# Turning v on VectorE and splitting the head scaling between ScalarE and GpSimd in a fused attention and mixture-of-experts layer

## The reference

```
def attn(x, W_qkv, W_out, s):               # x is (4, 512, 256), after a layer norm
    q, k, v = split(x @ W_qkv)              # 32 q heads, 8 k and v heads of 64
    q, k = rope(q), rope(k)
    a = q @ k.T / 8                         # per head, 512 x 512
    a = where((q_pos >= k_pos) & (q_pos < k_pos + 64), -inf, a)
    w = softmax(concat([a, sink]))[..., :-1]
    return (w @ v) @ W_out

x = x + attn(layernorm(x))
x = x + moe(layernorm(x))                   # 8 experts, top 2 of them, capacity 640
```

## Time and profile before

| what | value |
|---|---|
| median of 3 runs | 1060.13 us |
| lowest, highest | 1054.63 us, 1065.57 us |
| profiled execution, device time | 1057.24 us |
| its span, first to last instruction | 1055.5 us |
| mean granted TensorE clock | 0.993 of full speed |
| busy share: PE, DVE, ACT, POOL | 97%, 88%, 62%, 63% |
| one period (from one group's heads to the next group's) | 23.5 to 24.9 us |

### The profile page before, as it was taken

How to read it: one execution, slowest core, us unless ns; L and a number is a source line. 1 busy time by engine, 2 the same in 40 slices (tenths; PEclk the granted TensorE clock), 3 DMA queues, 4 the chain that set the end, 5 groups by cost and what they waited for, 6 DMA issues and landing times.

```text
span 1055.5 us, 32277 instructions
## 1 busy us (share of the span) xinstructions
PE 1024.9 (97%) x12943; PEld 720.9 (68%) x12943; DVE 926.8 (88%) x1967; ACT 655.0 (62%) x1671; POOL 665.1 (63%) x607
## 2 busy tenths in 40 slices
PE   7899999999999999999999999999988999999996
PEld 4466666666666666666666666666656999999995
DVE  6999999999999999999999999999985787777773
ACT  4666667666667766667776666776663555445551
POOL 6667776777666888666787777777752333333332
PEclk9999999999999999999999999999989999999998
DMA  3534544544333334333334334333424555555521
GB/s 112 142 108 118 137 131 140 132 112 135 93 83 83 96 99 111 99 104 81 80 95 114 100 103 121 98 83 96 119 70 162 119 119 123 117 123 124 101 46 21
DMA packets 155893, 112.10 MB, mean 106 GB/s; under 512 B 76480, under 2 KB 145152, under 8 KB 155616
## 3 DMA queue, kind: packets, MB, share of 16 engines
q1 hardware_dynamic: 137680, 90.03, 33.0%
q0 software_dynamic: 7296, 8.55, 4.8%
q10 hardware_dynamic: 10768, 11.46, 3.6%
HBM read 74.84 MB, written 21.83 MB: 92 GB/s over the span
## 4 chain that ended last, share of the span: by engine, by line
PE 56%; DVE 37%; issue 3%; ACT 1%; POOL 1%; DMA 1%; SPq 0%; POOLq 0%; DVEq 0%; ACTq 0%
PE bank L1586 22%; DVE probs_ring L1162 16%; DVE probs_t L1171 14%; PE bank L1562 10%; PE bank L1739 9%; PE bank L1750 6%; DVE heads_sb L1191 4%; PE bank L1753 3%; PE bank L1618 1%; PE bank L1508 1%; PE bank L1526 1%; PE bank L1533 1%; DVE neg_max L1162 0%; ACT probs_ring L862 0%; PE bank L1491 0%
## 5 line engine op out<-in xcount | busy, mean ns | idle before, releaser
L862 ACT ACTIVATE probs_ring<-probs_ring,neg_max 128x512 f32<-128x512 f32 x512 | 365.8, 717 | 210.3 <-DVE neg_max L1162 209.6
L1162 DVE CUSTOM_DVE_ANT_0 probs_ring<-bank,mask,sink_neg 128x512 f32<-128x512 f32 x512 | 360.1, 737 | 26.6 <-PE bank L1562 25.5
L1171 DVE STREAM_TRANSPOSE probs_t<-probs_ring 128x1024 f32<-128x1024 f32 x256 | 317.5, 1240 | 0.2 <-ACT probs_ring L862 0.2
L1562 PE MATMUL bank<-qk_st 64*128 64x512 f32 x1024 | 281.1, 625 | 11.9 <-DVE neg_max L1162 7.4
L1586 PE MATMUL bank<-probs_t,v_quads 32*64 32x256 f32 x8192 | 247.6, 381 | 0.1
L1586 PEld LDWEIGHTS bank<-probs_t,v_quads 32*64 32x64 f32 x8192 | 179.1, 132 | 76.5 <-issue 48.8
L691 POOL TENSOR_TENSOR chunk_sb<-chunk_sb,rope_sb 128x512 f32<-128x512 f32 (+1 forms) x94 | 120.0, 1276 | 103.9 <-issue 82.7
L810 POOL DMA_INDIRECT out<-expert_sb,slots x40 | 78.8, 1969 | 143.1 <-DVE expert_sb L1428 134.5
L1562 PEld LDWEIGHTS bank<-qk_st 64*128 64x128 f32 x1024 | 85.3, 186 | 77.4 <-DVE neg_max L1162 41.8
L696 POOL TENSOR_TENSOR qk_st<-chunk_sb,swap_sb 128x512 f32<-128x512 f32 (+1 forms) x94 | 120.2, 1279 | 7.4
L1618 PEld LDWEIGHTS bank<-wo_sb,heads_sb 64*128 64x128 f32 x992 | 96.1, 187 | 37.4 <-issue 29.2
(11 more groups left out here) (191 smaller groups left out, 1342.7 us busy)
## 6 DMA issues: line engine op xcount, KB each, us to landing
v_quads<-v_rows SPq DMA_DIRECT2D x128, 128.0 KB
recip_wide<-recip_rows SPq DMA_DIRECT2D x64, 256.0 KB
w_raw<-in_L_ffn_w SPq DMA_DIRECT2D x14, 1024.0 KB, 7.6
swap_sb<-chunk_sb SPq DMA_DIRECT2D x314, 32.0 KB
w_raw<-in_L_attn_W_qkv SPq DMA_DIRECT2D x32, 256.0 KB, 2.9
slot_rows<-x2T ACTq DMA_DIRECT2D x8, 662.5 KB, 5.8
slots_cut<-slot_rows SPq DMA_DIRECT2D x56, 80.0 KB, 3.0
w_raw<-in_L_attn_W_qkv SPq DMA_DIRECT2D x64, 64.0 KB, 2.7
```

What stands on the lines that cost most here:

```text
L862: nc.scalar.activation(probs[(g * UNITS + n) % RING][:, :], probs[(g * UNITS + n) % RING][:, :], ACT.Exp, bias=neg_max[j][:, n:n + 1], sca ...
L1162: nc.vector.tensor_tensor_reduce(probs[(g * UNITS + n) % RING][:, :], SCORE[SCORE_OF[n // 2][n % 2]][:, :], mask[:, L - P - t * P:2 * L - ...
L1171: nc.vector.transpose(probs_t[j][:, :, (h // 2) * (2 * P):(h // 2 + 1) * (2 * P)] .rearrange("p b (h q) -> p h b q", h=2)[:, :, :, t * BLK ...
L1562: nc.tensor.matmul(SCORE[SCORE_OF[n // 2][hh]][:, :], qk_st[j][half, h // 2, t * P:(t + 1) * P], qk_st[j][half, PAIRS, :], start=True, sto ...
```

## The change

Five things change in each period.

1. v is no longer turned by four PE transposes and copied by ACT. DVE turns it with one block transpose (`turn_v`, step -7, i.e. 9 of the period before) from `chunk_sb` into the unused upper half of `swap_sb[KV]`. The trip through DRAM now writes 1024 pieces of 32 floats in two DMAs, where it wrote 128 rows of 256 floats in one, and reads back rows of 1024 floats.
2. The heads of all groups but the last leave PSUM by four ACT copies; POOL then multiplies them by the broadcast reciprocals, in two instructions of 128 x 512. Each of the two lets one half of the heads go.
3. The rotation of Q01 on POOL is cut in two: the products stay at step 5 and the sum goes to step 10, behind the scaling of the heads.
4. y0 on PE begins with the first half of the heads and waits for the second half in its middle. The residual sums on POOL move from step 38 (6 of the period) to steps 42 and 43 (10 and 11).
5. The scatters on POOL go three at a time at r = 99 and 115 (step 3 of a period, ahead of the rotation of k), and the last two at 127, for the third batch at 118.

```diff
-        TURN_V_AT, V_NEXT_AT = -8, -7
-        ROT_AT = {2: Q23, -12: KV, -11: Q01}
+        TURN_V_AT = -7
+        ROT_AT, Q01_TIMES_AT, Q01_SUM_AT = {2: Q23, -12: KV}, -11, -6
...
-        Y_FIRST_OUT_AT, Y_OUT_AT, RESIDUAL_AT = 30, 31, 38
-        ODD_ORDER = (1, 0)
+        Y_FIRST_OUT_AT, Y_OUT_AT = 30, 31
+        RESIDUAL_AT = {42: 1, 43: 0}
...
-        SCATTER_AT = {89: (0, 1), 99: (2,), 105: (3, 4), 115: (5,), 121: (6, 7)}
-        ROUTE_STEPS = 122
+        SCATTER_AT = {99: (0, 1, 2), 115: (3, 4, 5)}
+        LAST_SCATTERS, LAST_SCATTERS_AT = (6, 7), (127, 127, 118, 127)
+        ROUTE_STEPS = 128
...
-                sp.dma_start(v_rows, v_next[:, :, :].rearrange("p t d -> p (t d)")).then_inc(s_v_out, 16)
+                for q in range(HD // BLK):
+                    sp.dma_start(v_rows.rearrange("j (b d) -> j b d", d=HD)[:, :, q * BLK:(q + 1) * BLK],
+                                 v_turned[q * BLK:(q + 1) * BLK, :].rearrange("j (b i) -> j b i", i=BLK)
+                                 ).then_inc(s_v_out, 16)
...
+                if n == HEADS_AT and g < GROUPS - 1:
+                    pool.wait_ge(s_recip_in, g * 32 + 32)
+                    for half in range(2):
+                        part = slice(2 * half, 2 * half + 2)
+                        pool.wait_ge(s_heads_raw, 2 * g + half + 1)
+                        nc.gpsimd.tensor_tensor(heads_sb[:, part, :], heads_sb[:, part, :], recip_wide[:, part, :],
+                                                ALU.mult).then_inc(s_heads, 1)
...
+                if n == HEADS_AT and g < GROUPS - 1:
+                    act.wait_ge(s_pv, g + 1 + 1)
...
+                    for a in range(QUADS):
+                        ins = nc.scalar.activation(heads_sb[:, a, :], PV[a][:, 0:2 * P], ACT.Copy)
+                        if a % 2 == 1:
+                            ins.then_inc(s_heads_raw, 1)
...
+            def turn_v(g):
+                dve.wait_ge(s_chunk_out, g * CHUNKS + KV + 1)
+                if g > 0:
+                    dve.wait_ge(s_v_out, g * 32)
+                nc.vector.transpose(v_turned, chunk_sb[KV][HD:P, :]).then_inc(s_v_turned, 1)
...
-                if n == HEADS_AT:
+                if n == TURN_V_AT and g > 0:
+                    turn_v(g)
+                if n == HEADS_AT and g == GROUPS - 1:
...
-                    pe.wait_ge(s_heads, 2 * g + (half if g == GROUPS - 1 else 1) + 1 + 1)
+                    pe.wait_ge(s_heads, 2 * g + half + 1 + 1)
...
+                            if half == 0 and second == 1:
+                                pe.wait_ge(s_heads, 2 * g + 1 + 1 + 1)
```

More of the change, by code:

```diff
@@ L437, in chunk_bank @@
             return PV[3] if c == KV else PV[1] if c == Q23 and g == 0 else PROJ
-        def turned_v_bank(g):
-            return PV[0] if g == 0 else PROJ
         def turned_bank(half, last):
@@ L689, in rotate, with rotate_sum @@
                 straight, swapped = chunk_sb[c][rows, :], swap_sb[c][rows, :]
-                base = before_group + (q - Q23) * ROT_STEPS
                 nc.gpsimd.tensor_tensor(straight, straight, rope_sb[rows, 0, :], ALU.mult).then_inc(s_pool, 1)
                 nc.gpsimd.tensor_tensor(swapped, swapped, rope_sb[rows, 1, :], ALU.mult).then_inc(s_pool, 1)
-                pool.wait_ge(s_pool, base + 2)
+            def rotate_sum(g, j, c):
+                q = g * CHUNKS + c
+                rows = slice(0, HD) if c == KV else slice(0, P)
+                pool.wait_ge(s_pool, before_group + (q - Q23) * ROT_STEPS + 2)
                 if q == Q23:
                     pool.wait_ge(s_rot, Q23)
-                nc.gpsimd.tensor_tensor(qk_st[j][rows, PAIRS if c == KV else c - Q01, :], straight, swapped,
-                                        ALU.add).then_inc(s_rot, 1)
+                nc.gpsimd.tensor_tensor(qk_st[j][rows, PAIRS if c == KV else c - Q01, :], chunk_sb[c][rows, :],
+                                        swap_sb[c][rows, :], ALU.add).then_inc(s_rot, 1)
             pool.wait_ge(s_small_in, 16)
@@ L703, in pool_step @@
                     rotate(g, j, c)
+                if n == Q01_TIMES_AT and g > 0:
+                    rotate_times(g, Q01)
+                if n == Q01_SUM_AT and g > 0:
+                    rotate_sum(g, j, Q01)
                 if n == (SECOND_SPLIT_AT if g == 1 else SPLIT_AT) and 0 < g < GROUPS - 1:
@@ L763, in pool_route @@
                                    channel_multiplier=1).then_inc(s_ids, 1)
-                for c in SCATTER_AT.get(r, ()):
+                for c in LAST_SCATTERS if r == LAST_SCATTERS_AT[b] else SCATTER_AT.get(r, ()):
                     if not last:
@@ L841, in chunk_out @@
                     act.wait_ge(s_rot, q - CHUNKS + 1)
-                if c == Q23 and g > 0:
-                    act.wait_ge(s_v_turned, g + 1)
+                if c == KV and g > 0:
+                    act.wait_ge(s_v_turned, g)
                 nc.scalar.activation(chunk_sb[c][:, :].rearrange("p (c a i) -> p a c i", a=QUADS, i=BLK),
@@ L992, in act_ahead @@
                     act.wait_ge(s_late, 1 if i < TPB else 2)
[L993 to L994 removed]
+                    if i > 0:
+                        act.wait_ge(s_norm_turned, TPB + i)
+                    nc.scalar.activation(xn1[:, :], x_sb[:, TPB + i, :], ACT.Identity,
                                          bias=bias_late[:, i:i + 1], scale=rstd_late[:, i:i + 1]).then_inc(s_norm, 1)
@@ L1487, in project @@
                 else:
-                    pe.wait_ge(s_v_next, g + 1)
+                    pe.wait_ge(s_chunk_out, g * CHUNKS + Q01 + 1)
+                    if g % NKV == 3 and g > NKV:
+                        pe.wait_ge(s_x2T, 2 * (g // NKV))
+                    if g % NKV == 4 and g > NKV:
+                        pe.wait_ge(s_centred, g // NKV)
+                    if g % NKV == 5 and g > NKV:
+                        pe.wait_ge(s_place, g // NKV)
+                    if g - 1 in LATE_PERIODS:
+                        pe.wait_ge(s_xT_lo, TPB + LATE_PERIODS.index(g - 1) + 1)
                 for kc in range(KC):
@@ L1513, in project_pair @@
                                 ins.then_inc((s_proj_part, s_proj)[second], 1)
-            def turn_v(g):
-                pe.wait_ge(s_chunk_out, g * CHUNKS + (Q01 if g > 0 else KV) + 1)
-                if g % NKV == 3 and g > NKV:
-                    pe.wait_ge(s_x2T, 2 * (g // NKV))
-                if g % NKV == 4 and g > NKV:
-                    pe.wait_ge(s_centred, g // NKV)
-                if g % NKV == 5 and g > NKV:
-                    pe.wait_ge(s_place, g // NKV)
-                if g - 1 in LATE_PERIODS:
-                    pe.wait_ge(s_xT_lo, TPB + LATE_PERIODS.index(g - 1) + 1)
-                for c in range(TPB):
-                    ins = nc.tensor.transpose(turned_v_bank(g)[:, c * HD:(c + 1) * HD],
-                                              chunk_sb[KV][HD:P, c * P:(c + 1) * P],
-                                              identity[HD:P, HD:P])
-                ins.then_inc(s_v_turned, 1)
             def keep_warm(count, bank, with_rows):
```

62 lines of the change are left out of this document (26 added, 36 removed).

## The result

The changed kernel takes 1101.41 us (median of 4 runs, 1098.9 to 1109.07), the kernel before 1060.62 us in the same comparison (4 runs). The ratio is 1.040, 95% interval 1.034 to 1.047: slower by 40.8 us. The profiled execution of the changed kernel is the slowest of its four: 1109.07 us, with a span of 1107.3 us against 1055.5. In all that follows T is the point at which the heads of a group begin to leave PSUM, and K the start of the rotation of k, counted from T.

What follows compares the result with a forecast made beforehand. PE was taken as the bound, with DVE adding 0.2 to 0.25 us a period. 1057.2 - 7.4 + 26.5 + 13.0 = 1089.3 us, as a median 1092; its case 1078 to 1102 (chance 0.45), range 1062 to 1112.

Steps and rivals of the forecast that it cites:

- Transposes, -7.4 us: On PE: dropping the four transposes of v saves 0.24 us for each of 31 groups, 7.4 us.
- DVE loses the heads: On DVE: 1.42 us of heads and a 0.51 us wait go, one transpose comes; PE's 0.23 us of waiting stay.
- POOL's chain, K + 8.91: On POOL: rotation of k, two Q01 products and two scalings make the heads' second half ready at K + 8.91.
- Stops, 26.5 us for 29 periods without the scatters' part: On PE at y0: waiting for the heads' second half costs 26.5 us over 29 periods, 0.9 us a period.
- K + 4.87: PE's stop at y0 in each period, where above zero, with T coming 0.24 us sooner.
- The 29 pairs: Readings of K in 29 periods of the kernel before: mean -4.0, extremes -5.8 and -2.5, not moved by the change.
- Three scatters, 13.0 us through K: On POOL: two more scatters ahead of k's rotation delay it 2.6 us in five periods, all reaching PE: 13.0 us.
- half swaps land sooner: Rival on SP's queue: K 1 to 2 us sooner cuts the stops, medians 1074 to 1065 us; chance 0.17.
- The heads in time: Rival: K at least 4.9 us before T, PE's work decides, medians 1046 to 1053 us; chance 0.08.
- It cancels: Rival: stops cost only 7 to 12 us and the transposes pay for them, 1057 to 1068 us; chance 0.12.
- The small pieces of v: Rival: v out flies 2 us past its cover, delaying Q23's half swaps, reciprocals and K: 1105 to 1120 us; chance 0.18.
- the signs of being wrong: k's rotation 5 us before PV's end; scaling under 1.2 us; v out above 5 us; PE's score waits growing.

Runs made afterwards that it cites:

- the heads-first kernel: Changed kernel with POOL's two products of Q01 placed behind the scaling of the heads instead of ahead: 1084.3 us, ratio 1.023.
- the one with k's swaps between: Changed kernel with k's half swaps between the reciprocals' two trips in SP's queue and scatters by threes at step 11: 1066.6 us, ratio 1.007.
- v on DVE alone: Kernel before with only v turned on DVE and sent through DRAM in small pieces; second residual sum one step later: 1069.21 us, ratio 1.009.
- the kernel before with three scatters: Kernel before with only the scatters changed, three at a time at r = 99 and 115: 1073.15 us, ratio 1.011.
- the scatters spread: Changed kernel with scatters two at a time at step 11 and one at step 3: 1086.94 us, ratio 1.027.
- v on PE: Changed kernel with k's half swaps between the reciprocals' trips and scatters at step 11, but v turned by PE's transposes in 1 KB rows: 1067.54 us, ratio 1.009.
- the kernel before with three off PV: Kernel before with scatters three at a time at step 11, not beside the products of probabilities and v: 1062.8 us, ratio 1.004.

## Why the prediction was right

The forecast was 1092 us, 1078 to 1102 for its case; 1101.41 is at that case's upper end. Taken by its own steps:

- **Transposes, -7.4 us:** right for a period, 0.24 forecast and 0.25 read. That 24 intervals sum to -7.3, close to the -7.4 forecast for 31 groups, is luck: at 0.25 they would give 6.0, and some intervals with routing work take up to 0.8 less.
- **DVE loses the heads:** right that it wins nothing. The transpose of v takes 0.71 us, where half of a 1024-wide one (0.62) was assumed.
- **POOL's chain, K + 8.91:** right to 0.2 us. Rotation 3.82 and both scalings 2.51 us in the period above; y1 starts at K + 10.7 in plain periods where 10.89 was forecast.
- **Stops, 26.5 us for 29 periods without the scatters' part:** the mechanism was right; that the sums agree for the 24 periods in which no scatters add to it, 17.6 forecast and 17.5 read, is partly luck. Period by period the two differ by 0.8 us on the mean. K came 0.26 us later than before on the mean of the 24, which alone would have made the sum 22.4, and each stop is 0.2 us shorter than K + 4.87. That y0's stop is on PE's own chain and nothing takes it up is shown from both sides by the heads-first kernel and the one with k's swaps between, where it is gone.
- **The 29 pairs:** they leave out the first period, in which PE stops for 6.5 us; the sum had nothing for this. K is +0.77 there (-2.41 before). With v on DVE alone K is +0.59 in it, so the new path of v makes it late: the two DMAs of v out land 4.58 and 4.89 us after their starts there, where the one DMA before took 2.51, and k's half swaps start at 50.88 instead of 48.46. It is not the path alone: with the heads first v out took 3.6 to 3.8 us there and K is -5.4.
- **Three scatters, 13.0 us through K:** here the mechanism was wrong. K does move, but T moves with it, since PV itself is slowed; the five periods' stops are 14.0 us (2.8 each, where 4 was named as a sign) and K + 4.87 + 2.6 gave 21.9. In its place stand 18.4 us of slowed PV in six intervals, which no term had, and which the kernel before with three scatters shows alone (16.3). The sixth interval, with five scatters, was not in the sum at all, and it has 7.2 of them.
- **Clock:** not in the sum. After the three longest stops y0 takes longer still. PE in the period of T = 384.61, and windows over it:

```profile
390.55 3.45 PE L1638 MATMUL bank<-wo_sb,heads_sb 64*128 64x256 f32 x16 [2.28 <-POOL heads_sb L738]
```

```profile
387.00:390.50 3.50, 1.27 (x5) 0.30 (x4) 3.45 (x8) 2.86 (x9) 3.50 (x4) 0.95 0.55 145
390.50:394.00 3.50, 3.45 (x18) 2.88 (x20) 0.39 (x1) 0.12 (x2) 3.50 (x3) 0.57 0.49 97
```

PE was busy for 1.27 us of 3.5, then ran at a mean granted clock of 0.57, most of the stretch at the 1.2 GHz level. y0 to y1 takes 4.14 us there, 3.07 in periods with shorter stops; over three periods, 3.7 us of the 38.1.

Between the heads of groups 0 and 30 the steps gave -7.4 + 39.5 = 32.1 us, and the trace has 49.2. The 17.1 between them are the slowed PV (18.4) and the first period (6.5), less the 7.9 us by which the five periods with scatters stopped less than forecast; the plain periods and the transposes add nothing. So two terms that no step had came to 24.9 us, and one that was 7.9 too large hid a third of it. The profiled execution lies 7.7 us above its own median, so against the median the forecast was 9 us short. That it fell into the range of its case owes something to this.

**The rivals.** That half swaps land sooner: the mean K was -3.67 over 29 periods, no sooner than -4.0. The heads in time: only with another order in SP's or in POOL's queue, and then other waits came. It cancels: no, 38.1 us of stops stand against 7.3. The small pieces of v: not in a plain period. SP of the changed kernel:

```profile
389.54 1.27 SPq L503 DMA_DIRECT2D v_rows<-swap_sb  x2
392.40 1.73 SPq L513 DMA_DIRECT2D v_quads<-v_rows  x4
```

v in starts 2.86 us after v out, under the 3.5 that I took, with 1.59 us between the end of v out's last start and it, the shortest of all 32 periods. With 1 KB rows in the same place (v on PE) the rows are:

```profile
469.27 0.34 SPq L507 DMA_DIRECT2D v_rows<-v_next  x1
470.99 1.75 SPq L515 DMA_DIRECT2D v_quads<-v_rows  x4
```

1.38 us, so at their shortest the 1024 pieces cost 0.21 us more in flight, beside one more DMA start. The Trainium skill (DMA: Bandwidth & Descriptors, Specifications) puts line rate at 512 bytes and up, and a read, modify and write below it; in plain periods these traces show at most those 0.21 us of it for two DMAs of 64 KB. The first period is where the rival may have come true: the longer flight of the two was 3.75 to 4.9 us in seven of the eight kernels with small pieces whose trace has it (2.6 in the eighth), and the one flight 2.4 to 2.8 in the four with 1 KB rows. The DMA engines are busy for 0.82 of that stretch, and no run tells the effect of the pieces' size from that of the traffic.

Of the signs of being wrong, one alone came, and once: a v out, at 140.62, took 5.54 us to land.

## What to carry to other kernels

Work moved to an engine with idle time is done when that engine's queue lets it, so look at what stands in front of it and what sets its start: here the order of two transfers in SP's queue was worth 24 us. Look as well at what stands behind it: with the heads first, the residual sums came late and PE waited for them through ACT. A wait inside an in-order queue (a scatter that waits for a broadcast, half swaps that wait for a copy) must be looked up again each time when the order of another queue is changed. Before an engine at 88% is given 0.7 us more a period, read which of its waits that fills and how long that wait is.

## What the runs showed of the hardware

Three indirect scatters of 128 rows in a row on GpSimd slow a stretch of small matmuls on TensorE: PV's piece of 96 takes 4.8 to 6.9 us instead of 2.85, with gaps of 0.5 us in the weight loads that no semaphore explains; part of the 6.9 ran at the 1.2 GHz level. Five of them made a piece of 80 take 7.55 us instead of 2.41. One scatter just ahead of such a piece does not slow it (in the kernel before one starts at 365.38, and the piece at 366.69 takes 2.85 us). One that starts with it costs 0.4 us (with the scatters spread, one starts at 404.56, and the piece at 404.54 takes 3.26 us). Three that run beside other work of TensorE cost little (ratio 1.004). Why is open, and a single such gap, 0.65 us, also stands in a piece of PV with no scatter near (ahead of 293.36 in the kernel before with three off PV).

After a stop in which TensorE was busy for 1.27 of 3.5 us, the granted clock was 0.57 over the next 3.5 us.
